# Merging the output weights into the key-value sums of a linear attention, with rows normalised by VectorE

## The reference

```
q = elu(x Wq^T) + 1,  k = elu(x Wk^T) + 1,  v = x Wv^T        (per head: T x 32)
kv = sum over t of k_t v_t^T                                  (32 x 32 per head)
z_t = 1 / (q_t . sum of k + 1e-6)
out_t = (q_t kv) z_t,  then  y = out Wo^T                     (512 x 512)
```

## Time and profile before

| | us |
|---|---|
| median of 3 runs (lowest, highest) | 930.83 (928.04, 932.05) |
| the profiled execution | 932.38 |
| its span | 930.6 |
| start of the feed-forward's first matmul in it | 227.59 |
| TensorE busy, of the span | 904.7 |
| VectorE busy | 651.8 |
| ScalarE busy | 400.4 |
| GpSimd busy | 297.5 |

### The profile page before, as it was taken

One profiled execution on the slowest core, in us unless ns is written; L12 is line 12 of the kernel. 1 busy time (PEld: TensorE's weight loads), 2 busy tenths in 40 slices (PEclk: granted clock), 3 DMA queues, 4 the chain that ended last, 5 costly groups with the idle time before them and its releaser, 6 DMA issues.

```text
span 930.6 us, 13844 instructions
## 1 busy us (share of the span) xinstructions
PE 904.7 (97%) x4976; PEld 720.5 (77%) x4976; DVE 651.8 (70%) x1256; ACT 400.4 (43%) x685; POOL 297.5 (32%) x266
## 2 busy tenths in 40 slices
PE   8998999998999999999999999999999999999995
PEld 7776887886788888888777767786867878888883
DVE  6765953477987798799679857977689886644423
ACT  6542122222444643544464576465544364322222
POOL 1000100001787344344334423131226332734342
PEclk9999999999999999999999999999999999999998
DMA  8533101201310000000010200010200543141411
GB/s 287 181 93 122 47 23 36 90 13 41 86 46 1 1 1 1 1 1 1 0 46 1 76 28 1 1 45 1 91 1 24 158 164 119 51 132 57 137 79 45
DMA packets 43973, 54.20 MB, mean 58 GB/s; under 512 B 6113, under 2 KB 25858, under 8 KB 43906
## 3 DMA queue, kind: packets, MB, share of 16 engines
q1 hardware_dynamic: 42082, 49.11, 16.3%
q0 software_dynamic: 1824, 4.22, 1.4%
HBM read 42.78 MB, written 10.52 MB: 57 GB/s over the span
## 4 chain that ended last, share of the span: by engine, by line
PE 63%; DVE 7%; issue 3%; ACT 2%; POOL 1%; DVEq 0%; ACTq 0%; POOLq 0%
PE ps L41 14%; PE ps L42 14%; PE ps L43 14%; PE ps L2336 8%; PE ps L2337 7%; DVE acc L1708 3%; PE ps L2441 1%; PE ps L2427 1%; PE ps L2368 1%; PE ps L2453 1%; PE ps L2434 1%; DVE junk L1911 0%; PE ps L2578 0%; PE ps L2524 0%; DVE state L1812 0%
## 5 line engine op out<-in xcount | busy, mean ns | idle before, releaser
L1708 DVE SCALAR_TENSOR_TENSOR acc<-ps,gu_scale,acc 128x512 f32<-128x512 f32 x264 | 197.3, 748 | 47.6 <-ACT acc L1369 27.8
L2336 PE MATMUL ps<-xt_hi,gu_val 128*128 128x512 f32 x352 | 140.5, 399 | 3.6 <-PEq L71 2.0
L2337 PE MATMUL ps<-xt_lo,gu_val 128*128 128x512 f32 x352 | 137.3, 390 | 0.0
L1369 ACT ACTIVATE acc<-ps,gu_scale 128x512 f32<-128x512 f32 x88 | 60.6, 689 | 94.1 <-PE ps L2337 94.0
L2241 POOL TENSOR_TENSOR fsg<-fsg,acc 128x512 f32<-128x512 f32 x44 | 59.4, 1349 | 108.3 <-DVE acc L1708 104.3
L2336 PEld LDWEIGHTS ps<-xt_hi,gu_val 128*128 128x128 f32 x352 | 66.0, 188 | 28.5 <-DVE acc L1708 10.9
L663 POOL TENSOR_TENSOR a_rstd<-a_var,minus_half 128x1 f32<-128x1 f32 x14 | 9.0, 644 | 210.7 <-DVE a_var L550 210.7
L2337 PEld LDWEIGHTS ps<-xt_lo,gu_val 128*128 128x128 f32 x352 | 66.1, 188 | 12.2
L2246 POOL TENSOR_TENSOR fh_lo<-fsg,fh_hi 128x512 fp32r<-128x512 f32 x44 | 58.9, 1340 | 42.6 <-ACT fh_hi L1381 42.6
L41 PE MATMUL ps<-dn_hi,fh_hi 128*128 128x512 f32 x176 | 69.2, 393 | 1.1 <-POOL fh_lo L2246 1.1
L42 PE MATMUL ps<-dn_hi,fh_lo 128*128 128x512 f32 x176 | 68.6, 390 | 0.0
(11 more groups left out here) (300 smaller groups left out, 2196.9 us busy)
## 6 DMA issues: line engine op xcount, KB each, us to landing
mw_raw<-in_w SPq DMA_DIRECT2D x16, 512.0 KB, 3.7
a_nib<-in_gate_up_packed SPq DMA_DIRECT2D x88, 64.0 KB, 2.5
x<-x SPq DMA_DIRECT2D x16, 256.0 KB, 2.8
mw_raw<-x SPq DMA_DIRECT2D x8, 512.0 KB, 4.2
out<-mw_raw SPq DMA_DIRECT2D x8, 512.0 KB, 3.8
xt_raw<-in_xT SPq DMA_DIRECT2D x3, 1024.0 KB, 5.5
x<-in_x SPq DMA_DIRECT2D x3, 1024.0 KB, 5.9
a_nib<-in_down_packed SPq DMA_DIRECT2D x8, 256.0 KB, 3.2
```

The source lines that it names most:

```text
L1369: act.activation(acc[part][u // 2 % 2][:, :], ps[:, FG, :], ACT.Copy, scale=gu_scale[:, part * IT + j, 0:1]).then_inc(s_g0, 1)
L1708: dve.scalar_tensor_tensor(out=a[:, :], in0=ps[:, FG + c, :], scalar=gu_scale[:, part * IT + j, c:c + 1], in1=a[:, :], op0=ALU.mult, op1=A ...
L2336: pe.matmul(ps[:, FG + c, :], gu_val[:, o, c, :], xt_hi[b % 2][:, c, :], start=True, stop=False)
L2337: pe.matmul(ps[:, FG + c, :], gu_val[:, o, c, :], xt_lo[b % 2][:, c, :], start=False, stop=True).then_inc(s_gu, 1)
```

## The change

The output weights are multiplied into the key-value sums once per pass: kv is laid out as four 128x128 blocks with zeros between heads (`kv_blocks`), transposed (`transpose_kv`), cut in parts (`kv_high`, `kv_low`) and multiplied with the output weights (`merge`, 4 groups of 3 matmuls), which gives a matrix M per group of heads (`m_hi`, `m_lo`). The rows' outputs are then q times M, so q itself is the stationary side, and numerators, division and transposes of `att` fall away. The normaliser of q is made for 512 rows at once by 16 small matmuls in four column tiles of the array (`normalisers`, 32x128), VectorE adds 1e-6 and takes the reciprocal (`inverse`), 16 matmuls in four row tiles spread it over each head's 32 partitions in four PSUM banks (`spread`), and VectorE multiplies q by it (`normalised`). q is then cut in parts by `query_high` and `query_low`, for 512 rows at a time.

Besides: the minimum with 1 in the queries goes (ScalarE takes Relu of -q, then the exponential of its negative); 14 of the 30 chunks are unpacked in pass 1 instead of 8; the low part of the third block of x is made by GpSimd; `transpose_rows` is split into four places that share one bank; the store of the scales stands ahead of chunk 16 in SyncE's list.

The core of the diff:

```diff
+Q_BANK = (2, 3, 2, 3)
+Y_BANK = ((0, 2, 3, 1, 0, 2, 3, 1), (2, 0, 3, 1, 2, 0, 3, 1))
...
-    for n in range(6, NGU):
+    for n in range(6, LATE_CHUNK):
         packed(n)
-    sp.wait_ge(s_q, KC)
-    block_of_xt(2)
     sp.wait_ge(s_dsp, 2)
     sp.dma_start(dn_parts[0], dn_scale_hi[:, :]).then_inc(s_dss, 16)
     sp.dma_start(dn_parts[1], dn_scale_lo[:, :]).then_inc(s_dss, 16)
-    sp.wait_ge(s_v, NGU)
+    packed(LATE_CHUNK)
+    packed(LATE_CHUNK + 1)
+    sp.wait_ge(s_v, LATE_CHUNK)
     rows_of(1, range(TB), s_xr[1])
-    packed(NGU)
-    packed(NGU + 1)
+    sp.wait_ge(s_q, KC)
+    block_of_xt(2)
     sp.wait_ge(s_q, 2 * KC)
     block_of_xt(3)
...
+        act.activation(e[:, :], ps[:, Q_BANK[m], :], ACT.Relu, scale=-1.0).then_inc(s_er, 1)
+        act.wait_ge(s_er, i + 1)
+        act.activation(e[:, :], e[:, :], ACT.Exp, scale=-1.0).then_inc(s_eq, 1)
+    def kv_high(b):
+        act.wait_ge(s_kvtp, b + 1)
+        act.activation(kvt_hi[b][:, :, :], ps[:, SMALL, :].rearrange("p (g n) -> p g n", g=KC), ACT.Copy).then_inc(s_kvh, 1)
+    def merged_high(b, g):
+        if b == 0:
+            act.wait_ge(s_dss, 32)
+        act.wait_ge(s_m, KC * b + g + 1)
+        act.activation(m_hi[b][g][:, :], ps[:, GROUP + g, :], ACT.Copy).then_inc(s_mh, 1)
+    def query_high(b, h, g):
+        act.wait_ge(s_qs, 2 * KC * b + KC * h + g + 1)
+        act.activation(q_hi[b][h][:, g, :], q[b][h][:, g, :], ACT.Copy).then_inc(s_qh, 1)
...
         query_exp(b, 1, 0)
...
+        if b:
+            rows_high(0)
         query_exp(b, 1, 1)
+        if b:
+            rows_high(1)
+        for g in range(3):
+            query_high(b, 0, g)
         query_exp(b, 1, 2)
+        if b:
+            rows_high(2)
+        query_high(b, 0, 3)
+        query_exp(b, 1, 3)
         if b == 0:
             x_high(2)
-        att_high(b, 2)
-        att_high(b, 3)
         if b:
...
+            rows_high(3)
+        for g in range(KC):
+            query_high(b, 1, g)
...
-            dve.wait_ge(s_num, NT * b + TB * h)
-        dve.scalar_tensor_tensor(out=query_out(b, h, m), in0=ps[:, Q_BANK[h][m], :], scalar=0.0, in1=e[:, :],
+        if h:
+            dve.wait_ge(s_m, KC * (b + 1))
+        dve.scalar_tensor_tensor(out=q[b][h][:, m, :], in0=ps[:, Q_BANK[m], :], scalar=0.0, in1=e[:, :],
                                  op0=ALU.max, op1=ALU.add).then_inc(s_qr, 1)
-    def sums(b):
+    def kv_blocks(b):
+        sums = ps[:, KV, 0:KC * (DH + 1)].rearrange("p (g e) -> p g e", g=KC)
+        mask = const.head_mask[:, :].rearrange("p (h e) -> p h e", e=DH)
+        dve.wait_ge(const.ready, 1)
+        dve.wait_ge(s_zero, b + 1)
         dve.wait_ge(s_kvt, NT * (b + 1))
...
+        dve.tensor_tensor(kv[b][:, :, :].rearrange("p g (h e) -> p g h e", e=DH),
+                          sums[:, :, 0:DH].unsqueeze(2).to_broadcast([P, KC, HG, DH]),
+                          mask.unsqueeze(1).to_broadcast([P, KC, HG, DH]), ALU.mult).then_inc(s_kvb, 1)
+        dve.tensor_tensor(k_sum[b][:, :, PAD:PAD + SEL], sums[:, :, DH:DH + 1].to_broadcast([P, KC, HG]),
+                          mask[:, :, 0].unsqueeze(1).to_broadcast([P, KC, HG]), ALU.mult).then_inc(s_ks, 1)
+    def kv_low(b):
+        dve.wait_ge(s_kvh, b + 1)
+        dve.tensor_tensor(kvt_lo[b][:, :, :], ps[:, SMALL, :].rearrange("p (g n) -> p g n", g=KC),
+                          kvt_hi[b][:, :, :].bitcast(F32), ALU.subtract).then_inc(s_kvl, 1)
+    def merged_low(b, g):
+        dve.wait_ge(s_mh, KC * b + g + 1)
+        dve.tensor_tensor(m_lo[b][g][:, :], ps[:, GROUP + g, :], m_hi[b][g][:, :].bitcast(F32), ALU.subtract).then_inc(s_ml, 1)
+    def inverse(b, h):
+        dve.wait_ge(s_z, 2 * b + h + 1)
+        dve.wait_ge(s_bc, 2 * b + h)
+        done(dve.tensor_scalar(inv[b][:, :], ps[:, SMALL, 0:P], 1e-6, None, ALU.add))
+        dve.reciprocal(inv[b][:, :], inv[b][:, :]).then_inc(s_zi, 1)
+    def normalised(b, h, g):
+        dve.wait_ge(s_bc, 2 * b + h + 1)
+        dve.tensor_tensor(q[b][h][:, g, :], ps[:, GROUP + g, :], q[b][h][:, g, :], ALU.mult).then_inc(s_qs, 1)
+    def query_low(b, h, g):
+        dve.wait_ge(s_qh, 2 * KC * b + KC * h + g + 1)
+        dve.tensor_tensor(q_lo[b][h][:, g, :], q[b][h][:, g, :], q_hi[b][h][:, g, :].bitcast(F32), ALU.subtract).then_inc(s_ql, 1)
+    def rows_low(c):
+        dve.wait_ge(s_fh, c + 1)
+        dve.tensor_tensor(xt_lo[0][:, c, :], ps[:, ROWS_T, :], xt_hi[0][:, c, :].bitcast(F32), ALU.subtract).then_inc(s_fl, 1)
+    def residual(b, t):
...
+        kv_blocks(b)
+        queries(b, 0, 0)
+        queries(b, 0, 1)
+        kv_low(b)
+        queries(b, 0, 2)
+        merged_low(b, 0)
+        merged_low(b, 1)
+        queries(b, 0, 3)
+        merged_low(b, 2)
+        merged_low(b, 3)
         queries(b, 1, 0)
...
+        inverse(b, 0)
+        if b:
+            rows_low(0)
         queries(b, 1, 1)
+        normalised(b, 0, 0)
+        normalised(b, 0, 1)
+        if b:
+            rows_low(1)
+        query_low(b, 0, 0)
+        normalised(b, 0, 2)
+        query_low(b, 0, 1)
         queries(b, 1, 2)
-        attend(b, 2)
-        attend(b, 3)
+        if b:
+            rows_low(2)
+        normalised(b, 0, 3)
+        query_low(b, 0, 2)
+        query_low(b, 0, 3)
+        queries(b, 1, 3)
+        if b:
+            rows_low(3)
+        inverse(b, 1)
         finish(b, 0)
-        att_low(b, 2)
-        finish(b, 1)
+        normalised(b, 1, 0)
+        normalised(b, 1, 1)
+        query_low(b, 1, 0)
+        residual(b, 1)
+        normalised(b, 1, 2)
+        query_low(b, 1, 1)
+        normalised(b, 1, 3)
+        query_low(b, 1, 2)
+        query_low(b, 1, 3)
+        statistics(b, 1)
         normalise(b, 0)
...
+        finish(b, 2)
         normalise(b, 1)
...
         finish(b, 3)
-        att_low(b, 5)
-        attend(b, 7)
         normalise(b, 2)
+        finish(b, 4)
         normalise(b, 3)
-        att_low(b, 6)
-        finish(b, 4)
-        if b:
-            att_low(b, 7)
         finish(b, 5)
         normalise(b, 4)
...
+    pool.wait_ge(s_xth, 3)
+    pool.tensor_tensor(xt_lo[0][:, :, :], xt_raw[0][:, :, :], xt_hi[0][:, :, :].bitcast(F32), ALU.subtract).then_inc(s_x2l, 1)
...
+    def transpose_kv(b):
+        pe.wait_ge(s_kvb, b + 1)
+        pe.wait_ge(s_r, NT * b)
+        for g in range(KC):
+            ins = pe.transpose(ps[:, SMALL, g * P:(g + 1) * P], kv[b][:, g, :], const.ident[:, :])
+        ins.then_inc(s_kvtp, 1)
+    def merge(b, g):
+        pe.wait_ge(s_wl[WO], 1)
+        pe.wait_ge(s_kvl, b + 1)
+        pe.wait_ge(s_k, NT * (b + 1))
+        pe.wait_ge(s_vr, NT * (b + 1))
+        three_products(pe, ps[:, GROUP + g, :], kvt_hi[b][:, g, :], kvt_lo[b][:, g, :], w_hi[WO][:, g, :], w_lo[WO][:, g, :],
+                       True, True).then_inc(s_m, 1)
+    def normalisers(b, h):
+        pe.wait_ge(s_ks, b + 1)
+        pe.wait_ge(s_qr, 2 * KC * b + KC * (h + 1))
+        if h == 0:
+            pe.wait_ge(s_kvl, b + 1)
+        else:
+            pe.wait_ge(s_zi, 2 * b + 1)
+        for t in range(TB):
+            for g in range(KC):
+                ins = pe.matmul(ps[g * DH:(g + 1) * DH, SMALL, 0:P], k_sum[b][:, g, PAD - SEL * t:PAD - SEL * t + DH],
+                                q[b][h][:, g, t * P:(t + 1) * P], start=(t == 0), stop=(t == TB - 1), skip_group_check=True)
+        ins.then_inc(s_z, 1)
+    def spread(b, h):
+        pe.wait_ge(s_sel, KC + 1)
+        pe.wait_ge(s_zi, 2 * b + h + 1)
+        if h == 0:
+            pe.wait_ge(s_ml, KC * (b + 1))
+        else:
+            pe.wait_ge(s_qs, 2 * KC * b + KC)
+        for t in range(TB):
+            for g in range(KC):
+                d = slice(g * DH, (g + 1) * DH)
+                ins = pe.matmul(ps[:, GROUP + g, t * P:(t + 1) * P], sel[d, t, :], inv[b][d, :], start=True, stop=True)
+        ins.then_inc(s_bc, 1)
+    def project_out(b, t):
+        h = t // TB
         if t == 0:
...
+            pe.wait_ge(s_ml, KC * (b + 1))
+        if t == b:
+            pe.wait_ge(s_ks, b + 1)
+            if b:
+                pe.wait_ge(s_fl, KC)
+        elif t == 1 - b:
+            pe.wait_ge(s_qr, 2 * KC * b + KC + 3)
+        elif t == 2:
+            pe.wait_ge(s_qr, 2 * KC * (b + 1))
+        elif t == 3:
+            pe.wait_ge(s_zi, 2 * b + 2)
         else:
...
+            pe.wait_ge(s_r, NT * b + t - 3)
         for c in range(KC):
-            ins = three_products(pe, ps[:, Y_BANK[t], :], at_hi[t % 2][:, c, :], at_lo[t % 2][:, c, :],
-                                 w_hi[WO][:, c, :], w_lo[WO][:, c, :], c == 0, c == KC - 1)
+            if t % TB == 0:
+                pe.wait_ge(s_ql, 2 * KC * b + KC * h + c + 1)
+            lhs = slice((t % TB) * P, (t % TB + 1) * P)
+            ins = three_products(pe, ps[:, Y_BANK[b][t], :], q_hi[b][h][:, c, lhs], q_lo[b][h][:, c, lhs],
+                                 m_hi[b][c][:, :], m_lo[b][c][:, :], c == 0, c == KC - 1)
         ins.then_inc(s_y, 1)
...
```

(29 more changed lines are left out.)

320 lines of the change are left out of this document (110 added, 210 removed).

## The result

The changed kernel takes 922.38 us (median of 5, 921.69 to 923.20), the kernel before 930.83 (928.04 to 932.05). The ratio is 0.991, with a 95% interval of 0.9895 to 0.9925: 8.45 us faster, where 11.3 were forecast (919.5). Repeated on another chip it gave 922.75 (921.43 to 923.98) against 931.48 for the kernel before, ratio 0.9908 (0.9892 to 0.9925).

What follows compares the result with a forecast made beforehand. TensorE, busy 904.7 of 930.6 us, was taken as the bound. 9.2 (pass 0) + 4.1 (pass 1) - 2.0 (stage's end) = 11.3 us, span 919.3, median 919.5; range 915 to 928.

Steps and rivals of the forecast that it cites:

- first feed-forward matmul at 216.3: End of the query stage: the feed-forward's first matmul was to start at 216.3 us, where before it started at 227.59.
- Pass 0: TensorE from its second query to the next pass's first `add_kv`: 61.3 us against 70.5, 9.2 us won.
- pass 1: TensorE from 169.51 to the end of its last projection: 51.8 us against 55.9, 4.1 us won.
- The small groups: Normalisers and spreading on TensorE: 1.0 and 0.95 us a group, 1.2 and 1.15 with the change of tile shape.
- the wait for the scales: Ahead of the first `att` transposes in pass 0: this pause (3.7 us) goes, as the scales are issued behind chunk 15.
- the pauses: New TensorE pauses in pass 0, behind VectorE's and ScalarE's work: 1.3 us in sum, each far below 3 us.
- rivals 1 and 3: Small tiles: row tiles multiply in turn, 9.8 us, 929.3 (chance 0.10); neither row nor column tiles overlap, 19.4 us, 938.9 (0.04).
- rival 4: First merged cut: scales late once more, pause over 3 us and low clock return, 4 to 5 us, 924; chance 0.03.
- 2.0 us back: End of the stage: VectorE and GpSimd end behind TensorE, the gap growing from 0.9 to 2.9 us.
- the feed-forward and what follows are unchanged: Everything from the feed-forward's first matmul to the end of the kernel was to take as long as before.
- from one execution to the median: Whole kernel: profiled execution 921.1 us, less the 1.55 by which before's stood above its median, gives a median of 919.5.
- Rival 2: Query phase: VectorE becomes the bound, 1 to 2 us more per half, some 5 in all, 924.5; chance 0.15.

## Why the prediction was right, and where it missed

**Right: the stage, in part by luck.** The step "first feed-forward matmul at 216.3" came out at 216.60. Pass 0 was forecast at 61.3 and took 61.23, pass 1 at 51.8 and took 51.88. The small groups cost 1.01 and 1.11 beside forecasts of 1.0 and 0.95, the wait for the scales is gone, and no pause in pass 0 is over 1 us. Within pass 0 two terms were off and cancel: the pauses were 0.5 (by the idle marks; 0.9 by the starts) and not 1.3, so what TensorE computes took 0.3 to 0.7 more than the 60.0 of the sum. And the start of the feed-forward came out within 0.3 because 0.67 that was not in the sum (the start) met a tail that was 0.45 better than forecast: that is luck.

**Right for its reason: overlap of small tiles (rivals 1 and 3).** One column tile costs 3.61 a group, one row tile 3.76. Both rivals' prices would have come about (10.4 and 10.6 where 9.6 and 9.8 were worked out) if the hardware had worked through its tiles in turn. It does not.

**Right: the early store.** Put back, the merged kernel loses 6.8 us; rival 4's price of 4 to 5 was too low. Counted from the first `add_kv` the feed-forward starts 7.2 later: the pause is 4.41, nine matmuls lose 0.2 each, and the normalisers, caught by the low clock, cost 1.86 instead of 1.01: 7.1.

**Right in kind, nearly in size: the tail.** "2.0 us back" at the stage's end was 1.55. GpSimd's last power ended 18.9 us behind the last spreading and not 19.3, since the nine instructions ahead of the second tile's statistics took 5.8 us and not 6.2. The reading that VectorE's rounds of 2.19 set the end was confirmed by giving them to ScalarE.

**Missed: "the feed-forward and what follows are unchanged."** It took 0.9 more. The forecast lengthened the wait ahead of it from 1.97 to about 4 and had read from the earlier trace rows that the clock falls behind such a pause, but did not put the two together. What the clock cost is 0.3 (12.60 instead of 12.26 to 12.28 to the first down projection). Another 0.3 stands behind TensorE's last matmul, which starts 12.1 us before the end of the span in the changed kernel (908.42 of 920.5) and 11.8 before it in the kernel before (918.81 of 930.6). Both repeat in the other profiles of these two forms to within 0.03, but the variants in which GpSimd normalises have 11.8; the cause is open. The last 0.3 lies between the two places and changes from execution to execution: the changed kernel repeated took 703.6 with the low clock, the one with ScalarE normalising 703.8 without it, and the kernel before 703.0 and 703.2.

**Missed: the start.** GpSimd's selection matrices stood in the list of added work nowhere, since GpSimd is idle there. They cost 0.7 us through VectorE, whose subtractions they slow. This was hidden in the total by the better tail.

**Missed: from one execution to the median.** The forecast took 1.55 us off, as the profiled execution of before stood that far above its median. The one of the changed kernel stands at its median. These 1.6 us, the 0.3 of the stage and the 0.9 of the feed-forward are the 2.9 between 919.5 and 922.38. The step that failed is to take the distance of one execution of before over to a kernel that no longer has the pause. Part of why before's profiled executions stand high is on record: the 53 executions by clock, above, differ by 3 us with how long the clock was low, and the pause that does this is gone in the changed kernel. The rest, 1.2 of the 1.55, stays open.

**Rival 2** (VectorE bounds the query phase, 924.5) would have been nearest in number, by 2.1 against 2.9, but not by mechanism: the one wait for VectorE that is marked in pass 0 is 0.29, the one in pass 1 ahead of the projections 0.66.

## What to carry to other kernels

When an edit has two parts, time each alone: here the store of two small transfers was worth more by itself (3.8) than the merged weights by themselves (2.0), and neither would have been known from the total. Where a bounding engine gets faster, look at who ends last at the next barrier. Where a pause makes the clock fall, find out how much of the loss falls into later waits (1.6 us became 0.3 here), and in how many executions it happens at all. Work given to an idle engine is not free: ask how long it takes there (the same normalise is 0.46 us on VectorE, 0.82 and two short steps on ScalarE, 2.08 on GpSimd) and what it slows beside it.

## What the runs showed of the hardware that was not expected

VectorE's subtraction of two tiles in SBUF and GpSimd's select, which reads SBUF, wait for each other. The single rows of the changed kernel:

```profile
7.31 0.73 POOL L720 TENSOR_SCALAR_AFFINE_SELECT a_sel<-a_sel 128x512 f32<-128x512 f32 x1
8.18 0.98 POOL L720 TENSOR_SCALAR_AFFINE_SELECT a_sel<-a_sel 128x512 f32<-128x512 f32 x1
```

```profile
7.45 1.11 DVE L619 TENSOR_TENSOR a_w_lo<-a_w_raw,a_w_hi 128x512 fp32r<-128x512 f32 x1 [1.76 <-ACT a_w_hi L440]
8.49 1.20 DVE L619 TENSOR_TENSOR a_w_lo<-a_w_raw,a_w_hi 128x512 fp32r<-128x512 f32 x1
```

Alone they take 0.69 and 0.73. The subtraction at 7.45 ends at 8.56, 0.52 behind the end of the select beside it (8.04); the select at 8.18 ends at 9.16, 0.60 behind the end of that subtraction; the next subtraction ends 0.53 behind that. The other seven profiles with the selection at the start show the same 0.53 and 0.59. GpSimd's normalise, beside VectorE's sums (one operand in PSUM) and statistics (one operand), slowed nothing: their 0.69 stayed. The Trainium skill (SBUF — State Buffer, Who interferes with whom) says that a VectorE instruction with two inputs in SBUF contends with a GpSimd instruction that reads SBUF, and that their shared port pair is an exclusive lock. The trace agrees on which pairs interfere, and the constant distance from the other's end is what a lock would give.

Three things more:

- The granted clock can fall with no idle time: behind one of four groups of 32-row matmuls in one row tile (3.76 us each) it was at its lower level for 3.4 us. Behind the same work spread over four row tiles, 1.11 us, it never fell.
- 128-column fp32 matmuls in four column tiles cost 0.032 us a record and in one 0.113; in four row tiles 0.035 and in one 0.118.
- Waits of 1.32 to 1.97 us ahead of the feed-forward left the clock up in six of seven profiles (the seventh is the one row tile, 1.95), those of 3.60 and more went with the lower level each time, for 3.4 us behind the five of 3.60 and 3.61, and for 6.8 us with the two of 5.99 and 6.00, within which it began.
